# Graph attention with layer norm: the turn of P and its shuffling transfers in two halves of column blocks

## The reference, cut to what matters

```
q = (x @ Wq).reshape(h, n, d); k = ...; v = ...
a = einsum('hnd,hmd->hnm', q, k) * d**-0.5
a = a + adj + adj
mask = adj == 0.0
a = softmax(where(mask, -1e6, a)); a = where(mask, 0, a)
out = einsum('hnm,hmd->hnd', a, v)
out = out.transpose(1, 0, 2).reshape(n, h * d) @ Wout
return layernorm(x + out)
```

## Time and profile before

| | |
|---|---|
| median of 3 executions | 1821.1 us (1816.62 to 1823.1) |
| the profiled execution | 1819.01 us, of this 1817.3 us span from first to last instruction |
| TensorE busy | 1791.5 us, 99% of the span |
| VectorE, ScalarE, GpSimd busy | 1097.2, 852.5, 983.7 us (60%, 47%, 54%) |
| granted TensorE clock | 0.998 |
| p_turned<-blocks transfers | 1532 by SP, 516 by ScalarE, 64 KB each |

### The profile page before, as it was taken

The page is one execution under the profiler, slowest core; times in us unless marked ns, Lnnn a source line. Parts: engine busy times, 40 slices in busy tenths (PEclk is TensorE's granted clock), DMA queues, the critical chain, the costliest instruction groups (busy, mean ns, idle before and its releaser), DMA issues.

```text
span 1817.3 us, 29365 instructions
## 1 busy us (share of the span) xinstructions
PE 1791.5 (99%) x10272; PEld 1580.1 (87%) x10272; DVE 1097.2 (60%) x2318; ACT 852.5 (47%) x1411; POOL 983.7 (54%) x762
## 2 busy tenths in 40 slices
PE   8999899999999999999999999999999999999998
PEld 7987789888998889988898888988889888998886
DVE  6888855555555655555555555555555555546666
ACT  5654555444544445444454444544454444544433
POOL 7878864444644455455564445644455455544443
PEclk9999999999999999999999999999999999999999
DMA  7888875666646666566665666656665566655664
GB/s 252 252 254 270 265 222 155 197 184 189 190 142 200 193 181 197 143 197 189 189 185 157 199 186 180 184 157 198 197 188 158 165 198 200 183 156 174 183 171 133
DMA packets 186995, 345.97 MB, mean 190 GB/s; under 512 B 39392, under 2 KB 96736, under 8 KB 170464
## 3 DMA queue, kind: packets, MB, share of 16 engines
q10 hardware_dynamic: 92032, 200.59, 35.4%
q1 hardware_dynamic: 94816, 143.50, 28.7%
HBM read 190.84 MB, written 18.87 MB: 115 GB/s over the span
## 4 chain that ended last, share of the span: by engine, by line
PE 85%; SPq 5%; DVE 2%; DMA 2%; issue 1%; ACTq 0%; POOL 0%; ACT 0%; DVEq 0%
PE bank L409 33%; PE y_bank L425 22%; PE bank L374 18%; PE y_bank L433 12%; SPq L313 4%; DMA p_turned<-blocks 2%; DVE blocks L683 1%; ACTq L590 0%; POOL p_split L491 0%; DVE y_acc L770 0%; SPq L292 0%; DVE p_split L776 0%; PE bank L394 0%; ACT p_split L562 0%; DVE y_acc L705 0%
## 5 line engine op out<-in xcount | busy, mean ns | idle before, releaser
L491 POOL TENSOR_TENSOR p_split<-p_turned,p_split 128x512 fp32r<-128x512 f32 x510 | 650.1, 1304 | 543.3 <-ACT p_split L562 542.8
L409 PE MATMUL bank<-k_split,q_split 128*128 128x512 f32 x3072 | 788.2, 392 | 3.9 <-DVE small L660 3.9
L409 PEld LDWEIGHTS bank<-k_split,q_split 128*128 128x128 f32 x3072 | 556.5, 189 | 106.1 <-DVE small L660 5.2
L425 PE MATMUL y_bank<-v_split,p_split 128*128 128x512 f32 x2048 | 546.4, 389 | 1.3 <-ACT p_split L562 1.1
L660 DVE CUSTOM_DVE_ANT_0 t_p<-bank,m_sb 128x512 f32<-128x512 f32 x512 | 351.6, 687 | 212.1 <-PE bank L409 183.7
L425 PEld LDWEIGHTS y_bank<-v_split,p_split 128*128 128x128 f32 x2048 | 383.7, 188 | 83.1 <-ACT p_split L562 2.4
L553 ACT ACTIVATE t_p<-t_p,small 128x2048 f32<-128x2048 f32 x128 | 256.9, 2007 | 359.6 <-DVE small L672 351.0
L480 POOL TENSOR_TENSOR w_slot<-raw_w,w_slot 128x512 fp32r<-128x512 f32 x192 | 250.1, 1304 | 252.0 <-ACT w_slot L533 248.9
L562 ACT ACTIVATE p_split<-p_turned 128x512 fp32r<-128x512 f32 x512 | 288.0, 620 | 109.1 <-DMA p_turned<-blocks 105.4
L683 DVE STREAM_TRANSPOSE blocks<-t_p 128x2048 f32<-128x2048 f32 x128 | 295.9, 2312 | 65.9 <-ACT t_p L553 46.5
L374 PE MATMUL bank<-x_t,w_slot 128*128 128x256 f32 x2304 | 306.3, 285 | 7.7 <-issue 4.9
(11 more groups left out here) (44 smaller groups left out, 619.2 us busy)
## 6 DMA issues: line engine op xcount, KB each, us to landing
m_sb<-m_dram ACTq DMA_DIRECT2D x112, 1024.0 KB, 5.3
p_turned<-blocks SPq DMA_DIRECT2D x1532, 64.0 KB, 2.2
p_turned<-blocks ACTq DMA_DIRECT2D x516, 64.0 KB, 2.9
blocks<-in_adj_dram SPq DMA_DIRECT2D x64, 256.0 KB, 4.2
raw_w<-in_L_gnn_Wv_dram ACTq DMA_DIRECT2D x64, 256.0 KB, 3.4
m_dram<-m_sb SPq DMA_DIRECT2D x16, 1024.0 KB, 6.5
raw_w<-in_L_gnn_Wq_dram ACTq DMA_DIRECT2D x63, 256.0 KB, 3.4
raw_w<-in_L_gnn_Wk_dram ACTq DMA_DIRECT2D x61, 256.0 KB, 3.8
```

What stands on the lines that cost most here:

```text
L409: mm = nc.tensor.matmul(dst[:], q[:, a, k, f * P:(f + 1) * P], k_split[:, kk, k, b * BANK:(b + 1) * BANK], start=(i == 0), stop=(i == len( ...
L425: nc.tensor.matmul(y[:], p_split[tau % 2][:, HI, j * P:(j + 1) * P], v_split[:, j].rearrange("p s d -> p (s d)"), start=(j == 0), stop=False)
L491: nc.gpsimd.tensor_tensor(lo, p_turned[:, i * BANK:(i + 1) * BANK].rearrange("p (j b) -> p j b", b=QUAD), hi.bitcast(F32), ALU.subtract).t ...
```

## The change

In all tiles but the last, `turn` becomes two instructions. The first turns column blocks 0 and 1 of the four (those that go to destination groups j = 0 and 1), the second 2 and 3. Each of the four `shuffled` semaphores becomes two, one for j = 0, 1 and one for j = 2, 3. The first half of the turn waits only for the first-half transfers of the tile whose buffer it takes, the second for the others. SP issues j = 0 and 1 of all four row groups after the first half of the turn, then j = 2 of all four after the second. ScalarE's copy of a row group waits for both of its semaphores. ScalarE's own transfers (j = 3) stay where they are and wait for both halves of the turn.

```diff
-        shuffled = [sem(f"shuffled{i}") for i in range(QUADS)]
+        shuffled = [[sem(f"shuffled{i}_{part}") for part in range(2)] for i in range(QUADS)]
...
+        def in_halves(tau):
+            return tau < ALL - 1
...
-                def shuffle(tau, i):
+                def shuffle(tau, i, columns):
                     if i == 0:
-                        sp.wait_ge(turned, tau + 1)
+                        sp.wait_ge(turned, 2 * tau + 1 if in_halves(tau) and columns.start == 0 else 2 * tau + 2)
                     if tau:
                         sp.wait_ge(p_lo, 4 * (tau - 1) + i + 1)
-                    for j in range(moved_by_sync(tau)):
+                    for j in columns:
                         sp.dma_start(p_turned[quad(j), i * BANK:(i + 1) * BANK],
-                                     turned_place(tau)[quad(i), j * BANK:(j + 1) * BANK]).then_inc(shuffled[i], 16)
+                                     turned_place(tau)[quad(i), j * BANK:(j + 1) * BANK]
+                                     ).then_inc(shuffled[i][j // 2], 16)
...
-                    for i in range(QUADS):
-                        if tau:
-                            shuffle(tau - 1, i)
-                        if i == 1 and t == LAST_Q and h + 1 < H:
-                            load_x(h + 1)
+                    if tau and in_halves(tau - 1):
+                        for i in range(QUADS):
+                            shuffle(tau - 1, i, range(0, 2))
+                            if i == 1 and t == LAST_Q and h + 1 < H:
+                                load_x(h + 1)
+                        for i in range(QUADS):
+                            shuffle(tau - 1, i, range(2, moved_by_sync(tau - 1)))
+                    elif tau:
...
-                    act.wait_ge(shuffled[i], 64 * (tau + 1))
+                    act.wait_ge(shuffled[i][0], 32 * (tau + 1))
+                    act.wait_ge(shuffled[i][1], 32 * (tau + 1))
...
-                        act.wait_ge(turned, tau + 1)
+                        act.wait_ge(turned, 2 * tau + 2)
...
-                    dve.wait_ge(exp_done, tau + 1)
-                    nc.vector.transpose(turned_place(tau)[:].rearrange("p (q j b) -> p j q b", q=QUADS, b=QUAD),
-                                        t_p[:].rearrange("p (j q b) -> p j q b", q=QUADS, b=QUAD)
-                                        ).then_inc(turned, 1)
+                    for part in range(2) if in_halves(tau) else (None,):
+                        if tau and turned_before(tau) is not None:
+                            for i in range(QUADS):
+                                for half in (part,) if part is not None else range(2):
+                                    dve.wait_ge(shuffled[i][half], 32 * (turned_before(tau) + 1))
+                        dve.wait_ge(exp_done, tau + 1)
+                        q = slice(0, QUADS) if part is None else slice(2 * part, 2 * part + 2)
+                        nc.vector.transpose(
+                            turned_place(tau)[:].rearrange("p (q j b) -> p j q b", q=QUADS, b=QUAD)[:, :, q],
+                            t_p[:].rearrange("p (j q b) -> p j q b", q=QUADS, b=QUAD)[:, :, q]
+                            ).then_inc(turned, 2 if part is None else 1)
```

More of the change, by code:

```diff
@@ L334, in _ @@
                             load_y(t // 2)
-                    for i in range(QUADS):
-                        if tau:
-                            shuffle(tau - 1, i)
-                        if i == 1 and t == LAST_Q and h + 1 < H:
-                            load_x(h + 1)
+                    if tau and in_halves(tau - 1):
[7 more added lines that the diff above has]
+                        for i in range(QUADS):
+                            shuffle(tau - 1, i, range(0, moved_by_sync(tau - 1)))
+                            if i == 1 and t == LAST_Q and h + 1 < H:
+                                load_x(h + 1)
                     if h == 0:
@@ L655, in score @@
                     if b == 0 and tau:
-                        dve.wait_ge(turned, tau)
+                        dve.wait_ge(turned, 2 * tau)
                     if tau < TILES and b == 0:
@@ L675, in turn @@
                 def turn(tau):
[L676 to L679, removed]
+                    if tau and turned_before(tau) is None:
                         dve.wait_ge(m_by_pool, len(by_pool))
                         dve.wait_ge(m_by_dve, len(by_dve))
-                    dve.wait_ge(exp_done, tau + 1)
-                    nc.vector.transpose(turned_place(tau)[:].rearrange("p (q j b) -> p j q b", q=QUADS, b=QUAD),
-                                        t_p[:].rearrange("p (j q b) -> p j q b", q=QUADS, b=QUAD)
-                                        ).then_inc(turned, 1)
+                    for part in range(2) if in_halves(tau) else (None,):
+                        if tau and turned_before(tau) is not None:
+                            for i in range(QUADS):
+                                for half in (part,) if part is not None else range(2):
[6 more added lines that the diff above has]
+                            ).then_inc(turned, 2 if part is None else 1)
                 def denominator(tau):
```

## The result

The changed kernel takes 1849.0 us (median of 6, 1838.1 to 1857.3) against 1820.3 us for the kernel before (6 runs of it by then): a ratio of 1.0151, 95% interval 1.0132 to 1.0171. It is slower by 1.5%, where 0.4% less had been forecast. Its runs also spread over 19 us, those of before over 6.5.

What follows compares the result with a forecast made beforehand. TensorE was taken to bound the kernel from 272 us, with VectorE late before that. 9.6 less 1.6 and 1.5 gave -6.5 us: 1812.5 or 1814.6, stated as 1813.5 us; own range 1810 to 1817.5, 8 in 10 range 1809 to 1822.

Steps and rivals of the forecast that it cites:

- at most 9.5 us to be had in the first head: TensorE's idle time between 82 and 240 us, about 9.5 us, is all that the shuffling can give back.
- the ring turn, issue, landing: First head, one shared buffer: turn, twelve SP issues, landing, next turn; 2.3 + 8.0 + 2.9 is 13.2 us a tile.
- the price of a half turn: VectorE pays one more fixed cost per split turn: 0.16 us, 1.6 us over ten turns.
- Where the change adds a wait: ScalarE's group 0 copy now needs column 2, issued later; at most 2.5 us delay, covered by 7.8 us in later heads.
- Rival B: Slower: group 0's copy waits on the previous tile's group 3 split; 11.0 or 14.3 us loop, about 1829; chance 0.14 with other losses.
- The term of -6.5 us: First head: VectorE reaches 212 us 6.5 us earlier, and TensorE leaves its weight wait there 6.5 us earlier.
- I therefore expect all nine waits, 9.6 us, to go: First head, 82 to 212 us: the turns' nine waits for shuffling transfers, 9.6 us in all, vanish.
- the time to the second half: First head: the second half of the buffer is out at 12.0 us and wanted at 14.2.
- rival D: SP, busy with the previous tile's loads, starts no earlier than now; about -4 us, chance 0.05.
- rival A: First head: the gain stays in SP and the DMA engines as issues and landings lengthen; -1.5 to -3, some 1817; chance 0.18.
- 1.5 us had been taken off: First head: allowance for SP's issues getting longer with a sometimes full queue, 1.5 us, 0 to 4 possible.
- The rule on the ports: Partitions 0 to 63 and 64 to 127 reach different port halves, so each phase would load one half; no size given.

Runs made afterwards that it cites:

- turn_halves_only: Changed kernel, but SP waits for the whole turn and issues the twelve transfers group by group; 1820.4 us, ratio 1.0001 against the kernel before.
- columns_02_13: Changed kernel with other halves: columns 0 and 2 first, then 1 and 3; 1851.6 us, ratio 1.0184 against the kernel before.
- later_heads_only: Kernel before with the change made from tile 14 on only, first head as before; 1847.0 us, ratio 1.0144.
- order_only: Changed kernel with the turn kept whole; only SP's new transfer order remains; 1875.5 us, ratio 1.0302 against the kernel before.
- before_light_adj: Kernel before, loading only 128 of each 512 columns of adj from tile 2 on, output not the reference's; 1812.2 us, ratio 0.9955.

## Why the prediction was wrong

**The reading of the kernel before held**: TensorE bound after 272 us, at most 9.5 us to be had in the first head, the ring turn, issue, landing there, the price of a half turn. TensorE did lose nothing by the split turn (`turn_halves_only`).

**The step that failed, and with it the sign**, is "Where the change adds a wait". It set a single delay, "at most the 4 issues, 2.5 us", against 7.8 us of cover. But the copy of group 0 frees, through GpSimd's split and SP's issue, the transfers that the next tile's copy waits for. Such a delay isn't paid once; it is a loop, and its whole length has to stay under TensorE's 11.75 us. Measured it is 13.0 to 13.4 in its plain rounds and 13.8 in the mean of the seven in the fifth head, so 1.3 us and more of the cover go per tile; the first late copy waits at 1013.87, and TensorE stops first at 1080.2, some six tiles later. Why no more is lost is only argued: over a whole head TensorE needs 223.11 / 16 = 13.9 us a tile, since some tiles carry many projections, and behind these the ring can come free again.

**Rival B was that ring, in the wrong place and with the wrong landing.** It was looked for in the first head and given 11.0 us without GpSimd's other work: three issues, a landing of 3.2, a copy, four splits. The link that was mis-sized is the landing. It was the median of the first head, where no m is loaded; in the later heads the 1 MB load goes out just before, and it is 5.6 us or more. Splits and issues were counted along another path, but to nearly the same sum: four splits and three issues, 5.26 + 1.9 = 7.2 us, where the chain goes through two splits (2.56) and then, since SP can't follow the splits, six issues before column 2 (4.1), 6.7 us. 0.7 + 2.56 + 4.1 + 5.6 is 13.0. What was said against B, that the splits come first in GpSimd's queue, holds and is beside the point. The trace of before held what was needed: ScalarE's last copy of tile 20 waits 2.25 us for its transfer, in a stretch where the load goes out with each exponential. That was read as covered, though it was the one group whose lateness the old order did not pass on to the others.

**The term of -6.5 us.** "I therefore expect all nine waits, 9.6 us, to go": 8.3 us of them stayed. The step that failed is the time to the second half, 12.0 us against the 14.2 at which it is wanted. Its parts were 1.2 us to SP's start, 7.6 for twelve issues and 3.2 for the landing; measured in the mean they are 2.6, 9.6 and (median) 3.7, 15.9 together. The start is rival D, SP is still busy with the loads; the issues are rival A, 0.9 us more a tile, 8 us over nine tiles, where 1.5 us had been taken off. With the change in that head alone the whole kernel is at 1.0010 (1.0000 to 1.0020), so by itself this part would have given no change. The ring of the kernel before was also added up with a landing of 2.9 us (2.3 + 8.0 + 2.9) that stands in no row; the rows have 3.44 and a median of 3.2.

**The rule on the ports** (the Trainium skill, SBUF — State Buffer, Door 1: The DMA port swizzle) had been put forward as a cause for rival A. `columns_02_13` spreads each phase over both halves of the partitions and is no faster, so no run here shows an effect of it. With the rule on the fixed cost of an instruction (the Trainium skill, VectorE: DVE Perf Modes, The TRN2 errata) the trace agrees: twice 1.229 us instead of 2.312, 0.15 us more.

What stays open: why in the profiled run heads five and eight fall into the ring and the others do not. The entry in head five is a late landing (ScalarE waits 3.49 us at 1013.87, on a transfer issued beside a load of m). It does not look like chance: the traces of `later_heads_only` and `columns_02_13` have the ring in the same two heads, and `order_only` in these and the third. How much the fifth head loses differs, 15.65 us in the changed kernel, 8.3 and 10.7 in those two, so at least a part of the spread of 19 us can lie there; only one run of this kernel has a trace.

## What to carry to other kernels

When an order makes the first consumer wait for the last producer of a round, don't weigh the delay against the slack once: add up the loop through the buffer that it closes (free, issue, landing, copy, free) and compare it with the time of the engine that bounds a round. Take the landing from the place where the transfer will be issued, with what is in the queues there, and at its late values, since one late round is enough to enter such a loop. And ask of the engine that issues whether it has a gap into which an earlier start can fall: SP had almost none here, at a DMA share of 0.86, and the time came back as longer issues.

## What the runs showed of the hardware

The issue of a transfer is not a constant: SP's 32x512 transfer took 0.59 us in the median, but up to 1.85 us (changed kernel, 96 to 202 us). Twelve took, in the mean of eight tiles of the first head, 8.7 us in the kernel before (DMA share 0.86) and 9.6 us in the changed one (0.88); with less of adj (0.71) it was 8.2 us in `before_light_adj`. A 64 KB transfer issued beside a 1 MB load landed in 5.5 to 7.4 us on the chain of the fifth head; the median of SP's transfers there (1000 to 1110 us) is 2.4. TensorE's granted clock was 0.59 of full in the 3.6 us after a wait of 3.1 us (1083.4 to 1087), and 1.00 in the 13 us behind it.
